# Attention on one core: where the negated row maxima are seeded from, the order of exponentials and seeds, and the place of the second maximum

## What is computed

```python
def _L1_attn_ref(x, Wq, Wk, Wv, Wo, bo):
    N_HEADS, HEAD_DIM = 16, 64
    b, s, _ = x.shape                      # 1, 2048
    q = (x @ Wq).reshape(b, s, N_HEADS, HEAD_DIM)
    k = (x @ Wk).reshape(b, s, N_HEADS, HEAD_DIM)
    v = (x @ Wv).reshape(b, s, N_HEADS, HEAD_DIM)
    dot = jnp.einsum('bihd,bkhd->bhik', q, k)
    w = jax.nn.softmax(dot / jnp.sqrt(jnp.float32(HEAD_DIM)), axis=-1)
    a = jnp.einsum('bhij,bjhd->bihd', w, v)
    return a.reshape(b, s, N_HEADS * HEAD_DIM) @ Wo + bo
```

## Time and profile before

| | us |
|---|---|
| median of 3 runs | 1858.48 |
| lowest, highest | 1855.24, 1868.66 |
| the profiled execution | 1866.86 |
| its span, first to last instruction | 1865.6 |
| PE busy (share of the span) | 1637.2 (88%) |
| DVE, ACT, POOL busy | 1302.3 (70%), 1154.1 (62%), 1306.1 (70%) |
| mean granted TensorE clock | 0.915 |

### The profile page before, as it was taken

One profiled execution on the slowest core, in us unless ns is written; L12 is line 12 of the kernel. 1 busy time (PEld: TensorE's weight loads), 2 busy tenths in 40 slices (PEclk: granted clock), 3 DMA queues, 4 the chain that ended last, 5 costly groups with the idle time before them and its releaser, 6 DMA issues.

```text
span 1865.6 us, 33807 instructions
## 1 busy us (share of the span) xinstructions
PE 1637.2 (88%) x12993; PEld 916.9 (49%) x12993; DVE 1302.3 (70%) x2075; ACT 1154.1 (62%) x1618; POOL 1306.1 (70%) x670
## 2 busy tenths in 40 slices
PE   3988863668999999999999999999999999995795
PEld 3767642654444444444444444444444444442475
DVE  2565667457777777777777777777777777763476
ACT  2455530355777777777777777777777777774323
POOL 2233331423998899998899998999998999995422
PEclk8587755778999999999999999999999999997698
DMA  8000000210000000000000000000000000000312
GB/s 244 3 3 4 3 1 8 61 44 1 1 1 1 1 1 1 1 1 1 1 1 1 1 1 1 1 1 1 1 1 1 1 1 1 1 1 25 101 40 74
DMA packets 33239, 29.72 MB, mean 16 GB/s; under 512 B 3676, under 2 KB 28752, under 8 KB 33080
## 3 DMA queue, kind: packets, MB, share of 16 engines
q1 hardware_dynamic: 24664, 19.38, 3.5%
q0 software_dynamic: 2496, 5.13, 0.8%
q10 hardware_dynamic: 5920, 3.04, 0.8%
HBM read 18.33 MB, written 9.21 MB: 15 GB/s over the span
## 4 chain that ended last, share of the span: by engine, by line
PE 61%; issue 12%; DVE 12%; ACT 7%; POOL 5%; DMA 1%; ACTq 1%; another core or an unknown queue 0%; POOLq 0%; DVEq 0%; SPq 0%
PE psum L1921 18%; PE psum L1906 13%; PE psum L1872 9%; DVE a_mx L2108 3%; ACT psum L2040 3%; POOL a_acc L2227 3%; PE psum L1887 2%; PE psum L1525 2%; PE psum L1929 2%; POOL y_rows L1090 1%; DVE a_Ql L2094 1%; PE psum L465 1%; ACT a_Qh L2002 1%; ACT a_Onh L2017 1%; PE psum L375 1%
## 5 line engine op out<-in xcount | busy, mean ns | idle before, releaser
L2227 POOL TENSOR_TENSOR a_acc<-a_acc,a_Pb 128x1024 f32<-128x1024 f32 x448 | 1065.8, 2379 | 108.4 <-ACT a_Pb L2025 52.7
L2108 DVE TENSOR_REDUCE a_mx<-psum 128x2 f32<-128x1024 f32 x512 | 622.0, 1217 | 194.6 <-PE psum L1872 191.4
L2025 ACT ACTIVATE a_Pb<-psum 128x1024 f32<-128x1024 f32 x512 | 496.8, 1023 | 296.3 <-PE psum L1906 291.1
L1921 PE MATMUL psum<-a_Pb,a_Vb 128*64 128x512 f32 x2048 | 494.1, 603 | 0.0
L2040 ACT ACTIVATE psum<-a_Mb 128x1024 f32<-128x1024 f32 x352 | 352.6, 1034 | 0.0
L1872 PE MATMUL psum<-a_Kh,a_Qh 64*128 64x512 f32 x1024 | 256.5, 491 | 26.1 <-DVE a_mx L2108 19.9
L1872 PEld LDWEIGHTS psum<-a_Kh,a_Qh 64*128 64x128 f32 x1024 | 103.1, 184 | 328.7 <-issue 305.6
L1921 PEld LDWEIGHTS psum<-a_Pb,a_Vb 128*64 128x64 f32 x2048 | 127.0, 136 | 222.5 <-issue 175.6
L1906 PE MATMUL psum<-a_Qh,a_Kh 64*128 64x512 f32 x1024 | 204.0, 394 | 1.8 <-ACT psum L2040 1.8
L1906 PE MATMUL psum<-a_Ql,a_Kh 64*128 64x512 f32 x1024 | 202.7, 390 | 0.0
L1906 PE MATMUL psum<-a_Qh,a_Kl 64*128 64x512 f32 x1024 | 202.7, 390 | 0.0
(11 more groups left out here) (389 smaller groups left out, 2013.8 us busy)
## 6 DMA issues: line engine op xcount, KB each, us to landing
x_rows<-att_raw ACTq DMA_DIRECT2D x2, 1483.5 KB, 25.4
g_w<-in_L_ffn_w_eDF_dram SPq DMA_DIRECT2D x2, 1408.0 KB, 8.7
r_W<-in_L_ffn_W_dram SPq DMA_DIRECT2D x1, 2048.0 KB, 14.1
r_tile_x<-x_rows SPq DMA_DIRECT2D x23, 64.5 KB
g_tile_x<-x_rows SPq DMA_DIRECT2D x23, 64.5 KB
y_all<-y_rows SPq DMA_DIRECT2D x4, 256.0 KB, 3.6
g_w<-in_L_ffn_w_eFD_dram SPq DMA_DIRECT2D x2, 512.0 KB, 9.4
g_xg<-y_rows SPq DMA_DIRECT2D x4, 256.0 KB, 3.9
```

What stands on the lines that cost most here:

```text
L1921: last = pe.matmul(ps[HEAD[h], B_O, :], b.Vb[:, p // 2 % 2, kc, at], b.Pb[:, step % BUFS, h * QT:(h + 1) * QT], start=(kc == 0), stop=(kc ...
L2025: act.activation(b.Pb[:, step % BUFS, :], ps[:, slot:slot + 2, :].rearrange("p a b -> p (a b)"), ACT.Exp, scale=SCALE).then_inc(S["probs"], 1)
L2108: v.tensor_reduce(b.mx[:, :, qc, quarter:quarter + 1], ps[:, bank:bank + 2, :], AX.X, ALU.max).then_inc(S[f"free{bank}"], 1)
L2227: g.tensor_tensor(b.acc[:, u, :], before, b.Pb[:, step % BUFS, :], ALU.add).then_inc(S["added"], 1)
```

## The change

- TensorE makes a seed for unit 0 alone. For units 1 to 31 SyncE stores the negated maxima (128 rows of 8 numbers) to a DRAM tensor in the order head, quarter, row, waits for it, and reads the 1,024 numbers back into all 128 rows of `b.Mb` (`attention_rows_sp`, placed ahead of the next layer's loads). VectorE's `negate` waits until the last store has read `b.nm`.
- ScalarE makes every seed but the first two of all. Its order becomes exponential of step s, seed of step s + 2, exponential of s + 1, seed of s + 3; VectorE makes none.
- TensorE's round: maximum, scores of two steps, odd jobs, second maximum, weighing.
- The jobs move: keys at step 1, queries at 3, sums at 4, output at 11, values at 14. The copy of the heads is at step 1, that of the normalised heads at step 8, VectorE's low part of the keys at step 2, inversions at 4 to 7, normalising at 8, its low part at 10.
- The maxima run further ahead: in unit 0 two on each of steps 0 to 6 (unit 1), and from step 9 on those of unit U + 2; `negate` comes at step 9 instead of in round 7.

Its core:

```diff
@@ -1672,51 +1672,44 @@
 NU = NT * P // QT
 PAIRS = 8
 UNITS = PAIRS * NU
-RN = NT // 2
-ROUNDS = UNITS * RN
-STEPS = 2 * ROUNDS
+STEPS = NT * UNITS
 BUFS = 8
 SCALE = 1.0 / float(np.sqrt(D))
 B_O, B_M, B_P = 4, 5, 7
 
 
-def misc_job(R):
-
-    U, d = R // RN, R % RN
+
+INVERT = (4, 5, 6, 7)
+
+AHEAD = 9
+
+
+def misc_job(step):
+
+    U, i = step // NT, step % NT
     p, qt = U // NU, U % NU
-    if d == 0 and p < PAIRS - 1:
+    if i == 1 and p < PAIRS - 1:
         return "k", p + 1, qt
-    if d == 1 and U:
+    if i == 3 and U < UNITS - 2:
+        return "q", U + 2
+    if i == 4 and U:
         return "sum", U - 1
-    if d == 4 and U < UNITS - 2:
-        return "q", U + 2
-    if d == 5 and U:
+    if i == 11 and U:
         return "out", U - 1
-    if d == 6 and p // 2 < PAIRS // 2 - 1:
-        return "v", p // 2 + 1, U % RN
+    if i == 14 and p // 2 < PAIRS // 2 - 1:
+        return "v", p // 2 + 1, U % 8
     return None
 
 
-def seed_job(R):
-    U, d = R // RN, R % RN
-    return ("seed", U + 1) if d == 7 and U < UNITS - 1 else None
-
-
-def max_jobs(R):
-
-    U, i = (R + 1) // RN + 1, (R + 1) % RN
-    return [("max", U, 2 * i + j) for j in range(2)] if U < UNITS else [None, None]
-
-
-
-SEED_DVE = (0, 5, 6, 7)
-
-
-def seeder(step):
-
-    if step % NT == 0 or step == 1:
-        return "pe"
-    return "dve" if step % 2 and (step // 2 - 1) % RN in SEED_DVE else "act"
+def max_jobs(step):
+
+    U, i = step // NT, step % NT
+    first = NT - AHEAD
+    if U == 0 and i < AHEAD:
+        jobs = [(1, 2 * i), (1, 2 * i + 1)] if i < first else [(1, first + i)]
+    else:
+        jobs = [(U + 2, i - AHEAD) if i >= AHEAD else (U + 1, first + i)]
...
@@ -1805,6 +1793,19 @@
     sp.dma_start(k.att_raw[:, 3, :].rearrange("p (a d) -> p a d", a=PAIRS), io["L1_attn_Wo"].rearrange("(a p) d -> p a d", p=P)).then_inc(S["att_w"], 16)
 
 
+def attention_rows_sp(k):
+
+    b, S, sp = k.a, k.S, k.nc.sync
+    for U in range(1, UNITS):
+        rows = k.max_rows[U % 2]
+        sp.wait_ge(S["negated"], U + 1)
+        sp.dma_start(rows.rearrange("h c p -> p h c"), b.nm[:, :, :].bitcast(F32), allow_slow_non_contiguous=True).then_inc(S["rows_out"], 16)
+        sp.wait_ge(S["rows_out"], 16 * U)
+        if U > 1:
+            sp.wait_ge(S["seeded"], seeds_of(NT * (U - 1) - 1))
+        sp.dma_start(b.Mb[:, U % 2, :], bcast(rows.rearrange("h c p -> (h c p)").unsqueeze(0), [P, 2 * QT])).then_inc(S["rows_in"], 16)
+
+
 def attention_weight_act(k, m):
     k.nc.scalar.wait_ge(k.S["att_w"], 64)
...
@@ -1873,54 +1874,47 @@
                              b.Kh[HEAD[h], p % 2, quarter * QT:(quarter + 1) * QT], start=True, stop=True)
         end(last, bank)
 
-    def seed(U):
-
-        pe.wait_ge(S["negated"], U + 1)
-        begin(("seed", U))
-        if U:
-            pe.wait_ge(S["probs"], NT * U - 1)
-        else:
-            pe.wait_ge(S["free2"], plan.before[2])
-        for first in ((0, 2) if U == 0 else (0,)):
+    def seed():
+
+        pe.wait_ge(S["negated"], 1)
+        begin(("seed", 0))
+        pe.wait_ge(S["free2"], plan.before[2])
+        for first in (0, 2):
             for h in range(2):
                 for qc in range(4):
                     last = pe.matmul(ps[:, first + h, qc * P:(qc + 1) * P], bcast(b.nm[:, h, qc:qc + 1], [P, P]), b.ident[:, :],
                                      start=(qc == 0), stop=(qc == 3), skip_group_check=True)
         end(last, 0)
 
-    def scores(R):
-        U, d = R // RN, R % RN
+    def scores(step):
+        U, kc, slot = step // NT, step % NT, 2 * (step % 2)
         p = U // NU
-        if d == 0:
-            freed(("seed", U))
+        if kc == 0:
             freed(("q", U))
             freed(("k", p, NU - 1))
-        for i in range(2):
-            kc, slot = 2 * d + i, 2 * i
-            at = slice(kc * P, (kc + 1) * P)
-            who, n = plan.seeded[2 * R + i]
-            if who != "pe":
-                pe.wait_ge(S[f"seeded_{who}"], n)
-            for n, (K, Q) in enumerate(((b.Kh, b.Qh), (b.Kh, b.Ql), (b.Kl, b.Qh))):
-                for h in range(2):
-                    last = pe.matmul(ps[:, slot + h, :], K[HEAD[h], p % 2, at], Q[HEAD[h], U % 3, :], start=False, stop=(n == 2), skip_group_check=True)
-            last.then_inc(S["scores"], 1)
-
-    def weigh(R):
-        U, d = R // RN, R % RN
+        if step == 0:
+            freed(("seed", 0))
+        if step > 1:
+            pe.wait_ge(S["seeded"], seeds_of(step))
+        at = slice(kc * P, (kc + 1) * P)
+        for n, (K, Q) in enumerate(((b.Kh, b.Qh), (b.Kh, b.Ql), (b.Kl, b.Qh))):
+            for h in range(2):
+                last = pe.matmul(ps[:, slot + h, :], K[HEAD[h], p % 2, at], Q[HEAD[h], U % 3, :], start=False, stop=(n == 2), skip_group_check=True)
+        last.then_inc(S["scores"], 1)
+
+    def weigh(step):
+        U, kc = step // NT, step % NT
         p = U // NU
-        if d == 0:
-            freed(("v", p // 2, RN - 1))
+        if kc == 0:
+            freed(("v", p // 2, 7))
             if U:
                 pe.wait_ge(S["heads_out"], U)
-        for kc in (2 * d, 2 * d + 1):
-            step = NT * U + kc
-            pe.wait_ge(S["probs"], step + 1)
-            for h in range(2):
-                at = slice((p % 2) * P + h * D, (p % 2) * P + (h + 1) * D)
-                last = pe.matmul(ps[HEAD[h], B_O, :], b.Vb[:, p // 2 % 2, kc, at], b.Pb[:, step % BUFS, h * QT:(h + 1) * QT],
-                                 start=(kc == 0), stop=(kc == NT - 1))
-            last.then_inc(S["weighted"], 1)
+        pe.wait_ge(S["probs"], step + 1)
+        for h in range(2):
+            at = slice((p % 2) * P + h * D, (p % 2) * P + (h + 1) * D)
+            last = pe.matmul(ps[HEAD[h], B_O, :], b.Vb[:, p // 2 % 2, kc, at], b.Pb[:, step % BUFS, h * QT:(h + 1) * QT],
+                             start=(kc == 0), stop=(kc == NT - 1))
+        last.then_inc(S["weighted"], 1)
 
     def sums(U):
...
@@ -1959,26 +1953,25 @@
         maximum(0, m)
         if m % 2:
             values(0, m // 2)
-    seed(0)
-    for _, U, m in max_jobs(-1):
-        maximum(U, m)
+    seed()
     for bank in range(NU + 1):
         pe.wait_ge(S[f"free{bank}"], plan.before[bank])
     pe.wait_ge(S["att_ready"], 1)
-    for R in range(ROUNDS):
-        late, early = max_jobs(R - 1)[1], max_jobs(R)[0]
-        if R and late:
-            maximum(*late[1:])
-        scores(R)
-        if early:
-            maximum(*early[1:])
-        if misc_job(R):
-            misc(misc_job(R))
-        if seed_job(R):
-            seed(*seed_job(R)[1:])
-        if R:
-            weigh(R - 1)
-    weigh(ROUNDS - 1)
+    for step in range(0, STEPS, 2):
+        for _, U, m in max_jobs(step):
+            maximum(U, m)
+        scores(step)
+        scores(step + 1)
+        for job in (misc_job(step), misc_job(step + 1)):
+            if job:
+                misc(job)
+        for _, U, m in max_jobs(step + 1):
+            maximum(U, m)
+        if step:
+            weigh(step - 2)
+            weigh(step - 1)
+    weigh(STEPS - 2)
+    weigh(STEPS - 1)
     sums(UNITS - 1)
...
@@ -2024,20 +2017,19 @@
             act.wait_ge(S["added"], adds_of(step - BUFS))
         act.activation(b.Pb[:, step % BUFS, :], ps[:, slot:slot + 2, :].rearrange("p a b -> p (a b)"), ACT.Exp, scale=SCALE).then_inc(S["probs"], 1)
 
-    def guard(U):
-        bank = begin(("seed", U))
-        if U > 1:
-            for who in ("act", "dve"):
-                act.wait_ge(S[f"seeded_{who}"], max(n for step, (w, n) in plan.seeded.items() if w == who and step < NT * (U - 1)))
-        act.activation(b.Mb[:, U % 2, :], ps[:, 0:2, :].rearrange("p a b -> p (a b)"), ACT.Copy).then_inc(S[f"free{bank}"], 1)
+    def guard():
+        bank = begin(("seed", 0))
+        act.activation(b.Mb[:, 0, :], ps[:, 0:2, :].rearrange("p a b -> p (a b)"), ACT.Copy).then_inc(S[f"free{bank}"], 1)
 
     def seed(step):
         U, slot = step // NT, 2 * (step % 2)
-        if plan.seeded[step][0] == "act":
-            bank, n = plan.at["seed", U]
+        if U:
+            act.wait_ge(S["rows_in"], 16 * U)
+        else:
+            bank, n = plan.at["seed", 0]
             act.wait_ge(S[f"free{bank}"], n)
-            act.wait_ge(S["probs"], step - 1)
-            act.activation(ps[:, slot:slot + 2, :].rearrange("p a b -> p (a b)"), b.Mb[:, U % 2, :], ACT.Copy).then_inc(S["seeded_act"], 1)
+        act.wait_ge(S["probs"], step - 1)
+        act.activation(ps[:, slot:slot + 2, :].rearrange("p a b -> p (a b)"), b.Mb[:, U % 2, :], ACT.Copy).then_inc(S["seeded"], 1)
 
...
@@ -2055,24 +2047,20 @@
     for qt in range(NU):
         keys(0, qt)
     queries(1)
-    for j in range(RN):
+    for j in range(8):
         values(0, j)
-    guard(0)
-    for R in range(ROUNDS):
-        U, d = R // RN, R % RN
-        probs(2 * R)
-        probs(2 * R + 1)
-        if seed_job(R):
-            guard(U + 1)
-        for step in (2 * R + 2, 2 * R + 3):
```

(68 more changed lines are left out.)

24 lines of the change are left out of this document (9 added, 15 removed).

## The result

| | before | after |
|---|---|---|
| median of the runs of one chip, us | 1858.53 (4 runs) | 1877.62 (4 runs) |
| span of the profiled execution, us | 1865.6 | 1876.3 |
| a full unit, start to start of GpSimd, us | 39.77 | 39.66 |
| unit 0, the same way, us | 38.76 | 52.80 |
| first to last unit start (31 units), us | 1222.38 | 1234.24 |

The ratio of the times is 1.0076, with a 95% interval of 1.0051 to 1.0101: the changed kernel is slower by 0.8%, some 14 us. The medians in the table differ by 19; in the later experiments the kernel before had medians of 1861.94 to 1865.86 us, so that its four runs here are on the low side. The units say where: unit 0 costs 14.0 us more, and the 30 after it give back 2.2 in all. (A full unit is given by the typical unit of pairs 0 to 5.

The account below looks back on a forecast made before the run. PE's own order was taken to set the attention unit (39.77 us), with GpSimd and ScalarE close behind. Full units 24, unit 0 11 and DMA rows 0 gave + 35 us on 1858.5: 1893 us, range 1850 to 1925.

Parts of the forecast that it names:

- within 1%: Whole kernel: forecast outcome class between faster by over 1% and slower, chance 0.20.
- the 24 for the full units: Attention's full units, pairs 0 to 6 but for unit 0: 27 units, each 0.88 us longer, 24 us.
- The floor of 38.20: PE's time for a full unit without the seed products (1.07) and one wait (0.50): 38.20 us.
- the 1.45 of waits behind ACT: PE waiting for seeds after rounds 3, 6 and 4: 0.45 + 0.45 + 0.55 = 1.45 us a unit.
- the 1.0 for bank 7: PE waits on the odd jobs' shared bank: queries 0.65, output 0.25, inversions filling DVE 0.1; 1.0 us a unit.
- The 11: Unit 0: six more pairs of maxima, + 11.5, less seed product and one wait, plus ACT waits: + 11 us net.
- the old 0.50 wait: PE's wait for DVE in the output's round before the change, 0.50 us a unit, forecast to go.
- x: ScalarE's wait for its own exponential to end before the seed: bounds 0 and 0.20, taken as 0.15 us.
- The rows by DMA (cost 0): Negated maxima through DRAM: store and read 10.5 us in a 14.5 us window, hidden with 4 to spare, cost 0.
- A: Rival: PE keeps its gain, new waits below 1.16 us a unit, 1829 us; chance 0.13.
- B: Rival: gain and waits cancel, x = 0, waits 1.2 to 1.8 us a unit, within 18 us of 1858; chance 0.17.
- C: Rival: DMA rows come late and stop ACT ahead of a seed, 31 times; + 62, 1955 us; chance 0.10.

Follow-up runs that it names:

- the first experiment: Changed kernel with ScalarE again running two exponentials, then two seeds, then its copies: 1859.85 us, ratio 0.9987 to the kernel before.

## Why the prediction was right or wrong

The direction and the range held, the size did not: + 35 us was forecast, and the medians differ by 19, the ratio says 14, the unit starts 12. By the ratio, + 0.8% with an interval up to 1.0%, the result lies in the "within 1%" that had a chance of 0.20. In the forecast's own sum (24 + 11 + 0) the step that failed is the 24 for the full units: they were to cost 0.88 us more each and cost 0.1 less. The floor of 38.20, the 1.45 of waits behind ACT and the 1.0 for bank 7 were all too high, by 0.38, 0.20 and 0.40. The 11 is nearly right. That the result lies in the range is owed to its width: the places of the waits were right, the sum of them was not.

**PE's floor (38.20), too high by 0.38.** The seed products and the old 0.50 wait went as said. "Reorders the same matmuls and is taken as 0" failed: the rounds with an odd job, other than the sums', run in 5.00 to 5.02 in the new order where they took 5.07 to 5.19 (the output's without its 0.50). Of this, 0.07 was a short gap of PE ahead of the queries' product, at 1179.54, 0.50 behind the maximum instead of 0.43; the prediction had called the 0.50 of the output's round the only wait. The kernel with the old order back shows that the move also carries the chain from ACT over DVE to the maximum, 0.7 us a unit in all.

**Waits behind ACT (1.45), too large by 0.2.** x was 0.09, not 0.15, and the round on ACT 4.14, not 4.24. Set against the rounds of the floor, PE loses 0.01 in round 3, 0.03 in round 4, 0.83 in round 5, 0.01 in round 6 and 0.37 in round 7, 1.25 together. The places were right (after rounds 3, 4 and 6), the weights not: the one behind the copy of the normalised heads took 0.83 instead of 0.55, the one after round 3 nearly nothing instead of 0.45. There the second scores did start 0.21 late, and lost 0.11 more because the first product after a pause lasts 0.34 instead of 0.23; but then the maximum followed after 0.80 in place of 0.88 to 0.92 and the weighing 0.34 behind it in place of 0.43, and the round ended on time. That short waits are given back at such switches is read from rows; what does it is not settled.

**Waits for bank 7 (1.0), too large by 0.4.** The queries' wait came at its place and nearly in its size, 0.53 in the row and 0.60 in the round against 0.65. The output's 0.25 and the inversions' 0.1 are not there: the output's lies wholly under the seed's wait until that one goes, as the first experiment showed, and I had added two waits of one engine that run at the same time.

**Together** 40.65 - 0.38 - 0.20 - 0.40 = 39.67, as measured. At 27 units this is 27 us of the forecast. (The last three of them, in pair 6, are 38.8 to 38.9 in both kernels.)

**Unit 0 (+ 11), right in kind, low by 3.** With the clock up a pair costs 1.94 us by its rows, against 1.92. I took six more pairs, which is what lies in unit 0 by GpSimd's starts, and subtracted the seed product and a wait. Two things were missing. The clock is low at its start (0.79 between 450 and 470 us, where before it was at 1.00), so that a pair costs 2.20 and the rounds around it run slower too: leaving the pairs out gave 13.4 back and not 11.5. And the maximum that opens round 1 stands directly behind the last of round 0 and waits 1.41 for it; that wait is there without the pairs too, where unit 0 takes 39.37 against 38.76 before.

**The rows by DMA (cost 0).** The cost was right: ACT waits 2.6 us in all. The margin was not: the store took 9.6 us, over the 9 that I had as its upper bound, and I had taken 5.5. The whole way took 13.8 in place of 10.5, inside the 7 to 14 but at their end, and 4 us to spare were 0.4. The reasoning by pieces (25.4 us for 5,888 long ones) had given 4.4 and, doubled, 9; the doubled one was the nearer. With a maximum two steps later the way turned into + 6.8 us a unit.

**The rivals.** A fell with the 1.85 of new waits, over its own 1.16 (+ 0.38 for the floor). B came nearest: it had 1.2 to 1.8 a unit, measured over my floor are 1.47, and the result lies at its edge of + 18. But its conditions were not met, x was not 0; it came true through a lower floor and waits that lie over each other. C did not come: the way took 13.8 us and the window was 14.2. That was close, and on the chip where the way takes 14.8 the runs do show ACT waiting in each unit. The 0.17 for B was too little: each of my terms had been taken near its upper end, and their sum had no term for overlap.

**The last pair (0)** holds: units there take 37.8 to 38.1 us in both, and PE waits at the end 6.57 us for GpSimd.

## What to carry to other kernels

When several new waits fall to one engine within a round, don't add them: a later one may lie under an earlier one, and taking the longer away buys only what sticks out; price each against the rounds without any wait, and remove them one after another until the next engine is full (here 39.66, 39.08, 38.43, 37.91 us). Put an operation that an in-order engine must do for the critical one ahead of, not behind, those that can wait for a third engine. A one-time cost at the start (a chain of maxima with one buffer, 1.92 us each) is paid once but fully, and can outweigh a gain per unit that is small. For a way of two transfers one behind the other, take the time of both from one and the same unit, not one unit's time of the first and the median of the second, and look at it on each chip before a wait for it is put down to an edit: 13.8, 14.3 and 14.8 us here, against a window of 14.2.

## What the runs showed of the hardware

- ScalarE starts an activation 0.09 us after the end of the one whose signal it waits for; without such a wait the next starts 0.91 after the start of a 1.03 us one, so the wait costs 0.2 of pitch.
- A store of 4 KB as 1,024 single numbers into DRAM took 8.3 to 10.8 us, the issuing engine's own row 0.36. The read of 512 KB behind it took 3.6 to 5.7 and was long where the store was short (8.4 and 5.1, 10.2 and 3.6), so that both together took 13.4 to 14.6; what couples them is not shown. The Trainium skill, Perfetto Trace Analysis, DMA Instruction — HWDGE (DVE, Sync), says that the signal follows the confirmed last write and that this can be surprisingly long towards HBM; no run here tells that share from the pieces'.
- On TensorE a change between products of different shape has its price in the order: 0.42 to 0.46 us from scores to a maximum, 0.43 from a maximum to a projection, 0.32 from scores to a projection or on to a maximum.
- After waits of 2.58 and 1.48 us the granted clock read 0.66 (between its levels of 1.2 and 2.4 GHz) and products took 0.79 instead of 0.50, though the unit was at 1.00 up to there.
